# A blocked triangular inverse kept as its transpose alone, in a test-time-training layer with a mixture of experts

## What is computed

```python
def step(carry, kvq):
    W, b = carry
    k, v, q = kvq
    g = 2.0 / d_h * (W @ k + b - v)
    W = W - LR * jnp.outer(g, k)
    b = b - LR * g
    return ((W, b), W @ q + b)

x = _layernorm(x + attn(x))          # the scan of step over each sequence
x = _layernorm(x + shared(x) + routed(x))
```

## Time and profile before

| | us |
|---|---|
| median of 3 runs | 2492.26 |
| lowest and highest | 2489.2, 2492.39 |
| the profiled execution's own time | 2490.89 |
| its span, first to last instruction | 2489.1 |
| one tile without scatters or routing | 52.7 |
| PE busy, share of the span | 91% |

### The profile page before, as it was taken

One profiled execution on the slowest core, in us unless ns is written; L12 is line 12 of the kernel. 1 busy time (PEld: TensorE's weight loads), 2 busy tenths in 40 slices (PEclk: granted clock), 3 DMA queues, 4 the chain that ended last, 5 costly groups with the idle time before them and its releaser, 6 DMA issues.

```text
span 2489.1 us, 40147 instructions
## 1 busy us (share of the span) xinstructions
PE 2271.5 (91%) x13154; PEld 1958.0 (79%) x13154; DVE 1529.8 (61%) x3594; ACT 875.6 (35%) x1887; POOL 1151.2 (46%) x1090
## 2 busy tenths in 40 slices
PE   6999999999999999999999999979578888999980
PEld 5888888888888888888888888768467777888770
DVE  5656665566655776655566676646534334778797
ACT  3333333333333333333333342223444434444440
POOL 1234433334333336543444533652555555666674
PEclk9999999999999999999999999989789989999995
DMA  4101111111111111111111111102533334788798
GB/s 158 34 35 40 40 41 39 47 35 43 43 35 47 39 35 43 43 35 43 43 35 43 43 35 39 48 9 81 196 97 129 117 105 156 259 274 286 241 357 280
DMA packets 101142, 233.29 MB, mean 94 GB/s; under 512 B 18128, under 2 KB 18768, under 8 KB 100176
## 3 DMA queue, kind: packets, MB, share of 16 engines
q1 hardware_dynamic: 72720, 152.48, 18.1%
q0 software_dynamic: 27936, 78.21, 9.7%
q10 hardware_dynamic: 288, 0.04, 0.0%
HBM read 141.22 MB, written 89.53 MB: 93 GB/s over the span
## 4 chain that ended last, share of the span: by engine, by line
PE 77%; DVE 8%; issue 4%; another core or an unknown queue 4%; ACT 3%; POOL 1%; DMA 1%; DVEq 1%; SPq 0%; ACTq 0%; POOLq 0%
PE banks L107 22%; PE banks L109 22%; PE banks L108 21%; PE banks L113 7%; PE banks L710 2%; PE banks L448 1%; DVE b_small L1609 1%; PE banks L547 1%; DVE b_Y L1056 1%; DVE xc L1056 1%; DVEq L1584 1%; DVE b_XL L1053 1%; PE banks L732 1%; DVE b_Y L1053 1%
## 5 line engine op out<-in xcount | busy, mean ns | idle before, releaser
L107 PE MATMUL banks<-W 128*128 128x512 f32 (+1 forms) x2040 | 753.7, 369 | 19.2 <-DVE W L1053 16.1
L109 PE MATMUL banks<-W 128*128 128x512 f32 (+1 forms) x2040 | 718.7, 352 | 0.0
L108 PE MATMUL banks<-W 128*128 128x512 f32 (+1 forms) x2040 | 716.7, 351 | 0.0
L107 PEld LDWEIGHTS banks<-W 128*128 128x128 f32 x2040 | 388.5, 190 | 71.9 <-POOL W L1659 15.0
L109 PEld LDWEIGHTS banks<-W 128*128 128x128 f32 x2040 | 387.4, 190 | 54.7
L108 PEld LDWEIGHTS banks<-W 128*128 128x128 f32 x2040 | 388.9, 191 | 50.9 <-issue 7.2
L1659 POOL TENSOR_TENSOR W<-S,W 128x512 fp32r<-128x512 f32 x256 | 327.4, 1306 | 112.6 <-ACT W L773 112.6
L773 ACT ACTIVATE W<-banks 128x512 fp32r<-128x512 f32 x320 | 191.2, 598 | 514.2 <-DVE banks L1053 232.9
L1659 POOL TENSOR_TENSOR X<-X,B 128x1024 f32<-128x1024 f32 x32 | 79.0, 2469 | 633.2 <-DMA X<-in_x 633.1
L773 ACT ACTIVATE W<-S 128x512 fp32r<-128x512 f32 (+1 forms) x288 | 180.1, 650 | 216.9 <-DVE S L1053 200.8
L1053 DVE TENSOR_TENSOR W<-banks,W 128x512 fp32r<-128x512 f32 x192 | 132.1, 688 | 169.9 <-ACT W L773 162.5
(11 more groups left out here) (158 smaller groups left out, 4454.8 us busy)
## 6 DMA issues: line engine op xcount, KB each, us to landing
RG<-ys SPq DMA_DIRECT2D x128, 256.0 KB
XT<-in_xT SPq DMA_DIRECT2D x32, 512.0 KB
X<-in_x SPq DMA_DIRECT2D x32, 512.0 KB, 3.5
x1d<-X SPq DMA_DIRECT2D x64, 256.0 KB
zd<-X SPq DMA_DIRECT2D x64, 256.0 KB, 2.0
b_Y<-zd SPq DMA_DIRECT2D x64, 256.0 KB
out<-b_Y SPq DMA_DIRECT2D x64, 256.0 KB
S<-in_we SPq DMA_DIRECT2D x32, 256.0 KB, 4.5
```

Of the source, the lines that this page charges most:

```text
L107: e.matmul(o, ll, rh, start=start, stop=False, skip_group_check=True)
L108: e.matmul(o, lh, rl, start=False, stop=False, skip_group_check=True)
L109: return e.matmul(o, lh, rh, start=False, stop=stop, skip_group_check=True)
```

## The change

The update of M itself is dropped at all levels: `inv_n` on PE makes only the products for the transpose, and `inv_n` on DVE subtracts 256 columns. Instead `inv_m` is done at each level (`inv_m(t, n)`): PE turns the transpose back, and ACT copies it to `k.MM[:, 0]`. `k.MM[:, 0]` has thus ACT as its only writer there. The spread product has 384 columns instead of 512 (`BLK`): rows 0 to 7 of each block keep 16 columns, rows 8 to 15 have their last 8; `k.R` is built by two DVE operations (`block_rows`), and `subst` reads accordingly.

The orders are changed to fit. On PE `down_x1` stands between `inv_m` and `inv_t`, and `qs_part` or half of `k_proj` between `inv_t` and `inv_n`. On DVE `down_x1` stands ahead of `inv_t`. On ACT the copy HH of the shared expert is now `half_x1`, and for the second sequence it stands behind the matrix copy `inv_m(t, 1)`.

```diff
-    def inv_m(t):
-        o = bank(w, ("MM", t), k.s_M0, t + 1)
-        w.wait_ge(k.s_M, NL * t + 1)
+    def inv_m(t, n):
+        o = bank(w, ("MM", t, n), k.s_M0, NL * t + n + 1)
+        w.wait_ge(k.s_M, NL * t + n + 1)
...
         for b in range(NB):
-            if not last:
-                mm(e, o[:, b * P:(b + 1) * P], k.MM[:, 1, b, :], k.T1[:, b, :])
-            z = mm(e, o[:, (2 + b) * P:(3 + b) * P], k.T1[:, b, :], k.MM[:, 1, b, :])
+            z = mm(e, o[:, b * P:(b + 1) * P], k.T1[:, b, :], k.MM[:, 1, b, :])
...
-        mm(e, o, k.cst[:, 2, :], k.R.rearrange("p i b j -> p (i b j)")).then_inc(k.s_Lb, 1)
+        mm(e, o[:, 0:BLK], k.cst[:, 2, :], k.R).then_inc(k.s_Lb, 1)
...
-        if n < NL - 1:
-            mmv = k.MM[:].rearrange("p k b n -> p (k b n)")
-            tt(mmv, mmv, o, ALU.subtract).then_inc(k.s_M, 1)
-            return
         mt = k.MM[:, 1, :, :].rearrange("p b n -> p (b n)")
-        tt(mt, mt, o[:, 256:512], ALU.subtract).then_inc(k.s_MT, 1)
+        tt(mt, mt, o[:, 0:256], ALU.subtract).then_inc(k.s_MT if n == NL - 1 else k.s_M, 1)
...
+        for h, o in enumerate(block_rows(k.R)):
+            rows = [P, HS, NB, (BS, HS)[h]]
+            own = unit_lr[:, h * HS:(h + 1) * HS].unsqueeze(2).unsqueeze(3)
+            tt(o, gd[:, :, h * HS:BS].unsqueeze(1).to_broadcast(rows), own.to_broadcast(rows), ALU.mult).then_inc(k.s_R, 1)
```

More of the change, by code:

```diff
@@ L27 @@
 LEVELS = [16, 32, 64]
+HS = BS // 2
+BLK = NB * HS * (BS + HS)
 NL = len(LEVELS)
@@ L635, in tensor_program @@
             qs_part(t, 0, 0)
-            inv_t(t, 1)
+            inv_m(t, 1)
             if t > 0:
                 down_x1(t - 1, 0)
-            else:
-                qs_part(t, 0, 1)
+            inv_t(t, 1)
+            qs_part(t, 0, 1)
             inv_n(t, 1)
-            if t > 0:
-                qs_part(t, 0, 1)
             k_turn(n, 0)
             k_proj(n, 1, 0)
-            inv_t(t, 2)
+            inv_m(t, 2)
             if t > 0:
                 down_x1(t - 1, 1)
-            else:
-                k_proj(n, 1, 1)
+            inv_t(t, 2)
+            k_proj(n, 1, 1)
             inv_n(t, 2)
-            if t > 0:
-                k_proj(n, 1, 1)
             qs_part(t, 1, 0)
@@ L666, in tensor_program @@
             down_x1(t - 1, 0)
+            inv_m(t, 1)
+            down_x1(t - 1, 1)
             inv_t(t, 1)
-            down_x1(t - 1, 1)
+            qs_part(t, 1, 0)
             inv_n(t, 1)
-            qs_part(t, 1, 0)
+            qs_part(t, 1, 1)
+            inv_m(t, 2)
             inv_t(t, 2)
-            qs_part(t, 1, 1)
             inv_n(t, 2)
@@ L809, in scores, with inv_m @@
         copy(k.ATp[0][:], kq).then_inc(k.s_AThi, 1)
[L811 to L814, removed]
+    def inv_m(t, n):
+        w.wait_ge(k.s_MM, NL * t + n + 1)
+        w.wait_ge(k.s_T, NL * t + n)
+        copy(k.MM[:, 0, :, :].rearrange("p b n -> p (b n)"), at["MM", t, n][:, 0:256]).then_inc(k.s_M0, 1)
     def inv_end(t):
@@ L1112, in subst @@
                 w.wait_ge(k.s_sub, n0 + 2 * j + b - 1)
-                stt(rest, lb[:, j, b, j + 1:BS], k.xc[:, b, j:j + 1], rest, ALU.mult, ALU.add).then_inc(k.s_sub, 1)
+                row = upper[:, j, b, j + 1:BS] if j < HS else lower[:, j - HS, b, j + 1 - HS:HS]
+                stt(rest, row, k.xc[:, b, j:j + 1], rest, ALU.mult, ALU.add).then_inc(k.s_sub, 1)
             yield
@@ L1479, in vector_program @@
             k_proj(n, 0)
+            if t > 0:
+                down_x1(t - 1, 0)
             tick()
@@ L1512, in vector_program @@
             down_x1(t - 1, 0)
-            inv_t(t, 1)
+            back_x1(t - 1, 1)
             split_w(1)
             down_x1(t - 1, 1)
+            inv_t(t, 1)
             inv_n(t, 1)
@@ L1518, in vector_program @@
             inv_t(t, 2)
+            inv_n(t, 2)
             split_w(4)
-            inv_n(t, 2)
             split_w(6)
```

34 lines of the change are left out of this document (21 added, 13 removed).

## The result

The kernel before takes 2490.42 us (median of 6 runs, 2486.07 to 2492.39), the changed one 2471.59 us (6 runs, 2464.43 to 2476.82): ratio 0.9927, 95% interval 0.9908 to 0.9946. Forecast were 2476.5 us and 0.9937, with a range of 2470 to 2484. The profiled execution of the changed kernel took 2472.85 us with a span of 2471.0, where before's took 2490.89 with 2489.1. To two digits the spans are 2489.05 and 2471.02, 18.0 apart.

A forecast was written before the change was run, and what follows sets the result against it. PE, 91% busy, was taken to bound the kernel. Tiles 1 to 28 save 18.5 us, less 0.8, 0.6, 0.7 and 1.2, plus 0.6: 15.8 off 2490.89; with 1.4 to the median, 2476.5 us, range 2470 to 2484.

The forecast's parts named there:

- The net of a tile: Middle tile on PE: products removed -0.88, transposes added +0.44, spread shrunk -0.22, net -0.66 us.
- The covers: Middle tiles: other PE work hides the new waits, with slacks of 1.0, 0.75 and 0.6 us.
- Scatter tiles: Tiles 18 to 25: PE's wait behind DVE's late subtraction grows some 0.1 each, +0.8 us in all.
- Routing tiles: Tiles 14 to 16 and 26 to 28: routing steps between the add and T, +0.6 us in all.
- Tile 0: First tile: both crossings bare, +1.4 against -0.66, net +0.7 us.
- Tile 31: Last tile: longer chain, later down_x1, and MTl behind two weight splits of 0.68, +1.2 us.
- Tiles 29 and 30: Tiles with 16 scatters each and held wake-ups: -0.6 us for both together, bounds -5 and +38.
- rival (a): Tiles 29 and 30: holds hit four new crossings, up to +37.6 us, kernel 2513; chance 0.08.
- (b): Each tile: T comes late and gives back 0.2 to 0.3 of the 0.66, 2482 to 2485 us; chance 0.09.
- (c): Tiles: another chain sets the period once PE is 0.66 shorter, about 2489 to 2492 us; chance 0.05.
- (e): Tiles: the clock falls, a tile having PE busy 57.28 instead of 52.67, about 2620 us; chance 0.01.
- (d): Each tile: transposes cost a product each, leaving only the spread's 0.22, 2487 to 2489 us; chance 0.01.

The follow-up runs named there:

- e5_bare: Changed kernel with inv_t of levels 1 and 2 directly behind the transposes in middle tiles, down_x1 behind it: 2388.47 against 2354.3 us, ratio 1.0149.
- b2_before: The kernel before itself, unchanged, run again for its trace; it fell on a chip with holds: 2478.8 us.
- e9_last_old: Changed kernel, but tile 31 inverts as the kernel before does, in the old orders: 2456.44 against 2472.98 us, ratio 0.9935.
- e1_last_order: Changed kernel, but in tile 31 DVE closes the inverse (MTl) ahead of the two weight splits: 2338.73 against 2354.3 us, ratio 0.9935.
- e6_last_chain: As e1_last_order, with inv_t of level 1 also ahead of the second down_x1 in tile 31: 2339.17 against 2354.38 us, ratio 0.9934.
- a2_after: The changed kernel itself once more, on a chip without holds: 2342.6 against 2354.38 us for the kernel before, ratio 0.9947.
- e4_spread_only: Kernel before with only the spreading product of 384 columns and R built in two blocks: 2347.31 against 2354.3 us, ratio 0.9970.

## Why the prediction was right, and where it was not

**The net of a tile** was right: -0.66 forecast, -0.68 seen. Its three prices hold apart too: spread 0.23 for 0.22, the exchange of products for transposes 0.45 for 0.44, and a transpose 0.10 for 0.11.

**The covers** were right to 0.03 us at each place, and each slack was there. What they are worth is what e5_bare shows: 1.5 us a tile.

**Scatter tiles**: the subtraction of level 0 is late as forecast, but takes 0.17 a tile from the gain and not 0.1. PE waits some 0.6 behind it (0.58 to 0.66 in the tiles looked at) where it waited 0.4. Between b2_before and e9_last_old the eight tiles gain 4.98 and not 3.94, so this term is uncertain by as much as its size. On the chips without holds it is nothing: tiles 18 to 25 last 52.02 there as well. **Routing tiles** lost 0.24 in all and not 0.6: 3.72 gained in six where 6 x 0.66 is 3.96.

**Tile 0**: the term of +0.7 was the right size for the tile and yet the measured difference is -0.65. In the first comparison the granted clock was 0.97 on the mean in before's tile 0 (a part of it at the lower level) and 1.00 in after's. With a full clock, in the second trace of the kernel before, tile 0 lasts 50.31, and in the changed kernel 51.16. In this order the rows are the profiled one of before, the second one of before, and after:

```profile
52.29:103.61 51.32, 51.31 (x287) 44.37 (x288) 33.67 (x83) 18.32 (x32) 16.57 (x15) 0.97 0.06 21
```

```profile
54.36:104.67 50.31, 50.01 (x287) 43.06 (x288) 33.66 (x83) 18.32 (x32) 16.59 (x15) 1.00 0.06 22
```

```profile
51.80:102.96 51.16, 49.79 (x283) 42.53 (x284) 33.13 (x84) 19.05 (x34) 16.58 (x15) 1.00 0.06 21
```

That is +0.85, two bare crossings of 0.75 less 0.66. The dip of the clock falls in the prologue in some executions and in tile 0 in others; start and tile 0 together end at 102.8 to 104.7 in all kernels alike. I had read one execution as if its state were the kernel's.

**Tile 31** is the term that failed: "I follow it to +1.2", where it was +6.45. The chain itself was followed well; up to DVE's last subtraction it is 0.7 longer (15.5 for 14.8), with the crossing of level 2 bare (PE waits 0.57) and the second down_x1 kept 1.21 by HL. What was mis-sized is the price of MTl's place: "two weight splits of 0.68 where one stood" took a price from a row in which POOL was idle. The term is 3.0 for the splits and some 1.5 for MTl itself, by e1_last_order and e9_last_old; with the 0.7 these are the 5.24. For the 1.2 that the tile loses behind MTl no cause is known: that stretch lasts 39.1 to 39.3 in the five traces in which the last tile inverts in the old way, and 38.7 to 41.2 in the nine others (40.4 and 39.8 in the changed kernel, 40.5 to 41.2 in the three with MTl ahead of the splits). It scatters only with the new orders, and no run tells by what. And the row that would have told was in the trace of before: POOL's add began 0.33 after MTl was done. The change moved it. DVE's second add of down_x1 ends at 10.5 in the old tile 31 and at 9.45 in the new one (1736.52 and 1712.97 less the tiles' starts), and POOL's add begins 5.6 behind it both times (5.75 to 5.94 in e1_last_order, e6_last_chain and e9_last_old). The kernel's code says why: in `sync_program` the load of X (`load_x`) waits for the store of both sequences' results (`store_z`), and the second store waits for this add.

**Tiles 29 and 30**: the seen -4.65 lies inside the term's bounds of -5 and +38, but the -0.6 taken was probably too small: 4.4 to 4.7 came again in the second comparison. The mechanism stands: the wake-ups are still held, now for the new crossing too. PE's transposes, ACT's copy and PE's next product of the changed kernel in tile 30, where ACT's idle time ends by nothing that is in the trace:

```profile
1646.96 0.41 PE L494 MATMUL banks<-ident,MM 128*128 128x128 f32 x2 [1.95 <-DVE MM L1068]
```

```profile
1654.91 0.38 ACT L776 ACTIVATE MM<-banks 128x256 f32<-128x256 f32 x1 [7.88 <-remote]
```

```profile
1655.44 1.19 PE L121 MATMUL banks<-MM,LT 128*128 128x128 f32 x4 [6.67 <-issue]
```

The transposes are done by 1647.4 and the copy starts at 1654.91. One crossing was held over 7 us and the tile did not grow: holds overlap, as rival (a) had against it. Rivals (b), (c) and (e) are out by the calm tile, (d) by the tile with doubled transposes. (The 2513 of rival (a) takes the 0.6 off where it had to be put back; 2514.7 is the sum.)

So the total was right through a sound middle and, by luck, through errors at the ends that nearly cancel: +5.2 in tile 31 against -4 in tiles 29 and 30, -1.4 at the start and -2.0 in the expert stage.

On a chip without holds the loss in tile 31 has little against it, and the ratio is 0.9947 rather than 0.9937. The tiles would give 14 us there (30 x 0.68 = 20.4, less 5.9 in tile 31 and 0.8 in tile 0, if the kernel before has its 52.70 there too, which no trace shows); 11.8 were measured. Of the rest no run shows the place. The expert stage took 606.2 in a2_after's trace, but its length seems to go with the chip: with the same code for it, 602.9 to 603.1 in three kernels on the chip of e4_spread_only, 604.9 to 606.2 in three on the chip of a2_after.

## What to carry to other kernels

A crossing PE to ACT to PE costs 0.75 us of PE when bare and nothing when 1.5 us of other products stand behind the transposes; an exchange of work that saves less than this pays only with its cover. Price a vector operation by the row of the same operation while the neighbour engine runs as it will then: look at what stands just behind it in the neighbour's list (here 0.33 us behind) before an operation is moved later. And a last iteration has no cover and its own critical chain, so keep the old form there if the new one only saves throughput.

## What was not expected of the hardware

DVE is slowed beside POOL when both add or subtract two operands in SBUF. W<-S,W on DVE, 0.68 alone, took 4.18 for two beside POOL, and MTl<-MM,MTh 1.48 to 2.21 where 0.43 is usual. POOL's add was no longer for it (2.34, against a mean of 2.46 on the page), its two splits were (3.38, against twice a mean of 1.31). The rows under "Tile 31" even give the size: each MTl that met POOL ended 0.27 or 0.28 after the end of the POOL operation beside it (1724.56 and 1724.28 in the changed kernel, 1693.50 and 1693.23 in e1_last_order, 1693.68 and 1693.40 in e6_last_chain), as if it had stood until then. What such a meeting costs is thus what is left of POOL's operation. An operation of DVE with one operand in PSUM paid nothing here. From the kernel before, DVE and then POOL:

```profile
1744.85 1.58 DVE L1053 TENSOR_TENSOR W<-S,W 128x512 fp32r<-128x512 f32 x1
1746.36 0.68 DVE L1053 TENSOR_TENSOR X<-banks,X 128x512 f32<-128x512 f32 x1
```

```profile
1744.60 2.96 POOL L1659 TENSOR_TENSOR W<-S,W 128x512 fp32r<-128x512 f32 x2
```

The split takes 1.58 beside POOL's two, and the add from PSUM, beside them as well, its usual 0.68.

The same kernel takes 2354 us on some chips and 2473 to 2491 on others. The changed kernel's calm tiles are alike on both, 52.02 at clock 1.00. The difference lies where indirect DMAs run: mostly 0.5 to 0.9 in tiles with 6 scatters, 8 to 15 in tiles with 16, and some 92 to 105 us in the expert stage (603 to 606 against 698 to 708), which gathers and scatters throughout. What differs between the chips, no run shows. A gain in such stretches is only seen over several executions.
